# A message-passing layer on one core: the edge attributes of a group loaded as five and five tiles instead of four and six

## What is computed

```python
row, col = (edge_index[0], edge_index[1])
tp = fctp_messages(node_features[col], edge_attr_tensor, W1, W2, W3, W4)   # bilinear in both inputs
messages = tp @ Wm + bm
agg = jax.ops.segment_sum(messages, row, num_segments=N_NODES)
upd = jnp.concatenate([node_features, agg], axis=-1) @ Wu + bu
return node_features + upd          # then x = _layernorm(x + this)
```

## Time and profile before

| | |
|---|---|
| median of 3 runs | 1809.12 us (1806.32 to 1816.49) |
| profiled execution | 1798.85 us |
| its span, first to last instruction | 1797.0 us |
| busy share of the span: PE, DVE, ACT, POOL | 88%, 87%, 54%, 61% |
| TensorE clock granted, mean | 0.962 |
| SyncE's queue (q1): MB, share of 16 DMA engines | 366.58 MB, 56.0% |
| GpSimd's queue (q0): MB, share of 16 DMA engines | 109.12 MB, 28.2% |
| DVE idle before `times_xv` (L555) / before `times_xs` (L543) | 77.9 us / 50.2 us |

### The profile page before, as it was taken

How to read it: one execution, slowest core, us unless ns; L and a number is a source line. 1 busy time by engine, 2 the same in 40 slices (tenths; PEclk the granted TensorE clock), 3 DMA queues, 4 the chain that set the end, 5 groups by cost and what they waited for, 6 DMA issues and landing times.

```text
span 1797.0 us, 35490 instructions
## 1 busy us (share of the span) xinstructions
PE 1576.2 (88%) x11572; PEld 874.3 (49%) x11572; DVE 1570.2 (87%) x1726; ACT 977.3 (54%) x2015; POOL 1097.9 (61%) x837
## 2 busy tenths in 40 slices
PE   4177889999999999999999999999999999388882
PEld 2033444544555555455555545545455554376662
DVE  6275789999999999999999999999999996299994
ACT  1123545555655555555555555555555555188884
POOL 3005777777777777777778777777777774211110
PEclk8688999999999999999999999999999999699996
DMA  9996578888888888888888888888888886899994
GB/s 377 399 392 176 137 229 237 245 245 250 249 243 256 242 241 250 244 258 242 251 249 242 244 246 250 247 240 243 251 240 244 239 253 170 289 400 420 414 420 156
DMA packets 174618, 477.23 MB, mean 266 GB/s; under 512 B 48664, under 2 KB 111640, under 8 KB 149484
## 3 DMA queue, kind: packets, MB, share of 16 engines
q1 hardware_dynamic: 91980, 366.58, 56.0%
q0 software_dynamic: 82304, 109.12, 28.2%
q10 hardware_dynamic: 288, 0.95, 0.2%
HBM read 380.25 MB, written 96.31 MB: 265 GB/s over the span
## 4 chain that ended last, share of the span: by engine, by line
DMA 38%; issue 25%; POOL 21%; DVE 10%; PE 2%; ACT 1%; SPq 1%; POOLq 1%; DVEq 0%; ACTq 0%
DMA agg<-summed,row_idx 24%; POOL agg L356 13%; POOL xg L338 7%; DMA prod<-agg 6%; DMA e_sb<-in_e_rep 4%; DMA agg<-start_rows 4%; DVE prod L555 3%; DVE prod L613 2%; DVE stats L632 2%; DVE prod L543 2%; DVE mv L638 1%; DMA xg<-in_x_rows,dst_sb 1%; PE ps L688 0%; ACT prod L498 0%; PE ps L676 0%
## 5 line engine op out<-in xcount | busy, mean ns | idle before, releaser
L356 POOL DMA_INDIRECT agg<-summed,row_idx x392 | 625.9, 1597 | 290.8 <-issue 150.5
L555 DVE TENSOR_TENSOR prod<-ps,e_sb 128x2048 f32<-128x2048 f32 x294 | 655.0, 2282 | 77.9 <-DMA e_sb<-in_e_rep 55.0
L695 PE MATMUL ps<-prod,packed_sb 128*32 128x512 f32 x2744 | 671.6, 606 | 0.8 <-ACT S_sb L410 0.8
L338 POOL DMA_INDIRECT xg<-in_x_rows,dst_sb x392 | 445.6, 1137 | 187.5 <-issue 103.6
L688 PE MATMUL ps<-prod,packed_sb 128*32 128x512 f32 x2352 | 396.4, 603 | 0.0
L563 DVE TENSOR_TENSOR prod<-ps,e_sb 128x3072 f32<-128x3072 f32 x98 | 328.0, 3347 | 0.0
L543 DVE TENSOR_TENSOR prod<-ps,e_sb 128x2048 f32<-128x2048 f32 x98 | 223.5, 2281 | 50.2 <-issue 31.3
L453 ACT ACTIVATE summed<-ps 128x644 f32<-128x644 f32 x98 | 69.4, 708 | 306.9 <-PE ps L753 303.4
L676 PEld LDWEIGHTS ps<-packed_sb,spread 128*128 128x128 f32 x1176 | 127.2, 142 | 199.5 <-DVE prod L555 95.3
L676 PE MATMUL ps<-packed_sb,spread 128*128 128x128 f32 x1176 | 173.5, 285 | 31.0 <-DVE prod L555 23.9
L498 ACT ACTIVATE prod<-prod,shift_n,rstd 128x160 f32<-128x160 f32 (+1 forms) x392 | 166.6, 507 | 42.3 <-DVE shift_n L625 42.3
(11 more groups left out here) (62 smaller groups left out, 1786.4 us busy)
## 6 DMA issues: line engine op xcount, KB each, us to landing
e_sb<-in_e_rep SPq DMA_DIRECT2D x98, 1536.0 KB
e_sb<-in_e_rep SPq DMA_DIRECT2D x98, 1024.0 KB
agg<-start_rows SPq DMA_DIRECT2D x49, 640.0 KB, 14.4
prod<-agg SPq DMA_DIRECT2D x48, 640.0 KB, 10.8
out<-prod POOLq DMA_DIRECT2D x48, 640.0 KB, 7.7
e_sb<-in_x_t SPq DMA_DIRECT2D x25, 640.0 KB, 11.1
prod<-in_x_t SPq DMA_DIRECT2D x24, 640.0 KB, 12.1
row_sb<-in_src_row SPq DMA_DIRECT2D x98, 128.0 KB
```

Source lines behind the costliest of these rows:

```text
L338: nc.gpsimd.indirect_dma_start(xg[g[1] % 2][:, q, :], None, x_rows, bass.IndirectOffsetOnAxis(dst_sb[g[1]][:, q:q + 1].bitcast(U32), 0)).t ...
L356: nc.gpsimd.indirect_dma_start(agg, bass.IndirectOffsetOnAxis(row_idx[g[1]][:, q:q + 1].bitcast(U32), 0), summed[g[1]][:, q // 2, q % 2 * ...
L555: nc.vector.tensor_tensor(prod[g[1] % 2][:, 4 + 4 * i:8 + 4 * i, :].rearrange("p (a b) e -> p a b e", b=2), ps[:, t_bank(g, 1 + i), :].uns ...
L695: return nc.tensor.matmul(ps[32 * quarter:32 * quarter + 32, S_BANK, :], w[:, 32 * half:32 * half + 32], prod[g[1] % 2][:, tile, :], start ...
```

## The change

Tile 4 moves from the second transfer of a group to the first. Both transfers then bring five tiles (1,280 KB). The first transfer's wait for the buffer goes from 4 to 6 products of the group two before, since tile 4 is read by `times_y` too. What VectorE waits for is left as it is: `es_in` before `times_xs`, `ev_in` before the first `times_xv`.

```diff
             def load_es(g):
                 if at_least(g, 2):
 
-                    sp.wait_ge(multiplied, number(g) * USES - 2 * USES + 4)
+                    sp.wait_ge(multiplied, number(g) * USES - 2 * USES + 6)
                     hold(sp, sp_passed)
...
-                sp.dma_start(e_sb[g[1] % 2][:, 0:4, :], e_rep[number(g), :, 0:4, :].unsqueeze(0).to_broadcast([32, 4, 4, GE])
+                sp.dma_start(e_sb[g[1] % 2][:, 0:5, :], e_rep[number(g), :, 0:5, :].unsqueeze(0).to_broadcast([32, 4, 5, GE])
                              ).then_inc(es_in[g[1]], 16)
...
-                sp.dma_start(e_sb[g[1] % 2][:, 4:ET, :], e_rep[number(g), :, 4:ET, :].unsqueeze(0).to_broadcast([32, 4, ET - 4, GE])
+                sp.dma_start(e_sb[g[1] % 2][:, 5:ET, :], e_rep[number(g), :, 5:ET, :].unsqueeze(0).to_broadcast([32, 4, ET - 5, GE])
                              ).then_inc(ev_in[g[1]], 16)
```

## The result

| | before | after |
|---|---|---|
| median, us | 1810.64 | 1819.10 |
| of runs, from and to | 8, 1806.24 to 1816.49 | 8, 1815.3 to 1824.28 |
| profiled execution and its span | 1798.85, 1797.0 | 1817.05, 1815.2 |
| ratio, 95% interval | | 1.0046 [1.0027, 1.0065] |

The change makes the kernel 0.46% slower, 8.5 us. Run again on another chip it gave 1.0078 [1.0054, 1.0103], so 8 to 14 us. The profiled executions lie 18 us apart, since the one of before took less time than any of the eight runs in its row; I read from them where time goes, and from the medians how much.

A forecast was written before the change was run, and what follows sets the result against it. VectorE was taken as nearly at its limit, 13.94 of 14.44 us a group, held by a chain of transfers and scatters. Terms 0 + 0 + 2 - 2 = 0 gave 1809 us, range 1786 to 1819.

The forecast's parts named there:

- the GpSimd one: Loop: the scatter pair lands 0.67 us later, but the third scatter's reply stays covered, so it costs nothing.
- +0.67 - 0.67 = 0, for 87 groups 0: Loop: second transfer issued 0.67 us later, takes 0.67 us less, lands when it did; no change per group.
- the first term: Loop: larger first transfer delays the scatter behind it, so the second transfer is issued 0.67 us later per group.
- The chain without VectorE: Loop: first transfer, scatter, second transfer, scatter follow one another, 7.27 + 7.76 us in the timeline read.
- the first rival: Scatter not held by the first transfer's tail; VectorE's 0.50 us a group gained, 43 us, to 1766; chance 0.18.
- The later wait in the loop: `load_es` needs `times_y`, about 4.3 us later, but the queue waits for scatters alone; cost 0.
- The cover: Slack of the third scatter's reply before SyncE is let go: 2.07 us at 402.00, 1.40 after the change.
- The tight slot: Slot at 817.61, where the scatter's reply has 1.29 us of cover, to become 0.62.
- this rival: GpSimd becomes late in the loop: 56 us at worst, 14 us if a quarter of groups, 1823; chance 0.12.
- The start: Before group 10 the later buffer wait binds and delays the start table: 0 to 4.3 us, taken as +2.
- The -2.0 for groups 6 to 8: Start: shorter second transfers let gathers go 0.67 us sooner at three ScalarE waits, gaining 2.0 us.
- my middle: Start: +2 us, taken between 0 and 4.3 us for the later table.

The follow-up runs named there:

- e10: Changed kernel (five and five tiles) with both VectorE additions cut to 4 of 512 columns: ratio 0.9895 to the kernel before.
- e14: Changed kernel with only the first VectorE addition cut to 4 of 512 columns: ratio 0.9928 to the kernel before.
- e15: Changed kernel with all its work, the first addition moved behind `times_y`: 1808.35 us, ratio 0.9981 to the kernel before.
- e9: Kernel before (four and six tiles) with both VectorE additions cut to 4 of 512 columns: ratio 0.9975 to the kernel before.
- e5: The changed kernel itself, run again on another chip: ratio 1.0078 to the kernel before.
- e4: Kernel before without the first transfer's wait for a scatter, so it goes out right behind the second: 1960.19 us, ratio 1.0871.
- e1: Kernel before, four and six tiles, with only the changed kernel's later buffer wait: 1806.76 us, ratio 1.0016.
- e3: Kernel before with eight and two tiles and the changed kernel's buffer wait: 1832.72 us, ratio 1.0168.
- e11: Changed kernel with DRAM rows padded to 12 tiles, the second half starting at tile 6: ratio 1.0301 to the kernel before.
- e12: Kernel before with its ten tiles at places 1 to 10 of the DRAM row: ratio 1.0041 to the kernel before.

## Why the prediction was wrong

**What failed.** The step is the GpSimd one, "Enough, and not by much", with a cost of nothing, and with it the sum "+0.67 - 0.67 = 0, for 87 groups 0". I moved GpSimd's scatters in time and took their durations along as constants, though the trace of before has gathers of 0.98 and 1.98 us side by side. With the additions cut the first term is as I had it and the second larger: 6.76 + 7.71 goes to 7.44 + 6.91, +0.68 and -0.80, a sum of -0.12 us a group. The change would then gain 0.8%, where I had nothing. With them it is +0.84 and -0.60, a sum of +0.24 in the profiled pair. So the change is a small gain from the transfers and a larger loss from the additions, which cost 0.25% with four and six tiles and 1.5 to 1.9% with five and five. The shift puts more of GpSimd's instructions into the additions (100 for 50). That the loss reaches the loop through these, since the chain hangs on scatters, is my reading: e10, e14 and e15 agree with it, and six and four tiles below don't. That VectorE can hold GpSimd up is in the Trainium skill, "SBUF — State Buffer", section "SBUF: two separate sides": a VectorE operation with two inputs in SBUF and a GpSimd operation that reads SBUF exclude each other for a whole instruction. The traces agree for GpSimd's side: a gather that begins 0.11 us into a 1.22 us addition is 0.98 us longer, one that began 0.08 us ahead of it is not, and beside the products, which have one input in `ps`, none is. They don't show the other side: in before and after 50 additions of 128x1024 began while a gather was under way, and none took over 1.23 us. I had read the page for transfers and not for this.

**Where in a slot it stands.** By the means over the 78 slots the changed kernel takes 14.64 us and e10 14.35. Of the 0.29 us between them 0.15 lie between the first transfer's issue and the slot's first scatter (1.06 us, with the additions 1.21): GpSimd comes late to it. 0.05 follow until SyncE is let go, and 0.04 and 0.06 in the same two pieces around the second transfer. With four and six tiles (before against e9) the first half changes by 0.04 only; the third scatter starts 0.33 us later, and the wait for it to land is 0.43 us shorter, so nothing is lost.

**What stays open.** Why that wait gets shorter with four and six tiles and not with five and five. In slots behind a stretched fourth scatter the first-to-second distance is 7.75 us against 7.56 in the others, but in e5 it is 7.63 against 7.50 and the whole slot 14.52 against 14.63, so no stretched scatter can be given a price. Six and four tiles have 73 stretched gathers and lose nothing; so the count doesn't decide it. Nor do the additions explain by themselves why cuts at 4.5 and 5.5 tiles are slower than both neighbours. The runs show the additions' part for whole tiles alone.

**What held.** The chain without VectorE: e9 takes 11% of VectorE's work away and the loop is no shorter (14.48), e4 takes the spacing away and loses 156 us. VectorE waits for the second transfer: from its issue to the first `times_xv` it was 7.15 us, now 6.49 (7.32 and 6.51 in the slots where VectorE waited), so it lands 0.7 to 0.8 us sooner after its issue, about as I had it. It is issued too late for that to count.

**The room there was.** I called VectorE the engine at its limit, with 13.94 us of 14.44. The earlier trace rows has TensorE busier, 1220.90 / 87 = 14.03. So the first rival could have gained no more than 0.41 us a group, 36 us and not 43, by the profile's modelled ends of matmuls.

**The later wait in the loop.** "It waits for scatters alone" is wrong as a reading of the queue, since it waits for `times_y` first (85 times, 194.6 us). The cost of 0 holds: the issue comes 4.0 us after `times_y` ends in the mean and never less than 2.9, in e1 as in the changed kernel, and e1's time allows 0.35% at most.

**The cover.** With 3.75 us for the reply (e3) instead of 4.57 it was 2.9 us in the slot of 402.00, not 2.07. The tight slot was less tight than I wrote, and this rival did not come about: GpSimd's waits for landed scatters, which it had over 1.3 us a slot longer, are 98.2 us in the loop before and 92.7 us after. That the outcome lies between the forecast and its 14 us is chance.

**The start.** Group 4's and 5's transfers went out at 96.64 and 114.99 (97 and 115.4 forecast), GpSimd's first scatter at 136.25, 2.06 us later than before (+2 forecast). The -2.0 for groups 6 to 8 did not come: ScalarE's three waits, as in the earlier trace rows, are

```profile
161.78 1.49 ACT L398 ACTIVATE spread<-xg 128x1536 f32<-128x1536 f32 x1 [6.40 <-DMA xg<-in_x_rows,dst_sb]
...
180.46 1.49 ACT L398 ACTIVATE spread<-xg 128x1536 f32<-128x1536 f32 x1 [7.84 <-DMA xg<-in_x_rows,dst_sb]
...
197.75 1.49 ACT L398 ACTIVATE spread<-xg 128x1536 f32<-128x1536 f32 x1 [6.48 <-DMA xg<-in_x_rows,dst_sb]
```

together 20.72 us, and the three of before were 20.72 too. The second got longer by what the others gave. The start repeats badly: `load_ev` of group 9, the first one held by scatters, went out at 221.56 before, at 221.75 and 216.61 in the two executions of the changed kernel, at 214.43 in e15. A lone profiled execution tells nothing there of less than 5 us. Both terms were below that, so the +2 that came out is no proof of my middle.

**The size.** The median is 10 us above the forecast, and 0.1 us above the range. Of the 10, 1.5 are the reference: the median of before is 1810.64 over eight runs and was 1809.12 over three. As I had no case in which the move costs 0.1 to 0.15 us a group, the upper end stood on the start and on the rival with the tight slot alone.

## What to carry to other kernels

Before instructions of an engine are moved in time at a constant duration, look whether that duration is constant in the trace. A group whose mean lies between two sizes (1137 ns for gathers of 980 and up to 2,000) says that something else decides, and the list of what runs beside each tells what; then ask where the change puts them. Where a chain runs through transfers and GpSimd's indirect ones, a VectorE operation with both inputs in SBUF is best placed, and tried in two places, against that chain and not against VectorE's own work. Here one place was right for five and five tiles and wrong for four and six.

## What the runs showed of the hardware that I had not expected

- A gather's issue on GpSimd is 0.98 us alone and up to 2.0 us when a VectorE addition of 128x1024 between SBUF tiles has just begun; the second scatter of a pair 1.58 us, and 1.85 when it begins 0.29 us into one of 128x512. Products with one input in `ps` don't do it. The additions themselves keep their 1.21 to 1.23 us when they begin beside a gather.
- The first scatter of a pair lets SyncE go 3.76 us after it starts behind a transfer of 0.5 MB issued 1.31 us before it, while 6.64 us passed at 402.00 in the earlier trace rows behind one of 1.5 MB.
- Two transfers of 1.5 and 1 MB issued 0.92 us apart instead of 7.6 made the kernel 8.7% slower, with the same bytes.
- Rows in DRAM 24,576 instead of 20,480 bytes apart went with +2.2% (five and five, e11 over e5, on two chips) and +0.4% (four and six, e12), with the same values read. The cause is open.
